# Second cross attention: a pair's residual, moments and normalisation on ScalarE and GpSimd instead of VectorE

## The reference, cut to what matters

```python
def _L1_xattn_ref(x, context, ln_gamma, ln_beta, w_q, w_kv, w_out, b_out, gate):
    xn = _layernorm(x, ln_gamma, ln_beta)
    q = (xn @ w_q).reshape(B, SQ, 16, 64)
    k, v = jnp.split(context @ w_kv, 2, axis=-1)      # then split into 16 heads
    attn = softmax(einsum('bqhd,bkhd->bhqk', q * SCALE, k))
    out = einsum('bhqk,bkhd->bqhd', attn, v).reshape(B, SQ, INNER)
    out = out @ w_out + b_out
    return out * jnp.tanh(gate[0])

x = _layernorm(x + _L1_xattn_ref(x, ctx_1024, ...))
```

## Time and profile before

| what | value |
|---|---|
| device time, median of 3 runs | 1886.55 us (1885.76 to 1887.1) |
| the profiled execution: device time / span | 1884.88 us / 1883.0 us |
| PE busy | 1667.1 us (89%) |
| DVE busy | 1549.9 us (82%) |
| ACT busy | 1275.3 us (68%) |
| POOL busy | 925.5 us (49%) |
| first to last `maximum` (L2217) of this phase | 603.7 to 1676.4 us |

### The profile page before, as it was taken

How to read it: one execution, slowest core, us unless ns; L and a number is a source line. 1 busy time by engine, 2 the same in 40 slices (tenths; PEclk the granted TensorE clock), 3 DMA queues, 4 the chain that set the end, 5 groups by cost and what they waited for, 6 DMA issues and landing times. The chain is left out here.

```text
span 1883.0 us, 34675 instructions
## 1 busy us (share of the span) xinstructions
PE 1667.1 (89%) x10425; PEld 1009.4 (54%) x10425; DVE 1549.9 (82%) x2885; ACT 1275.3 (68%) x2106; POOL 925.5 (49%) x723
## 2 busy tenths in 40 slices
PE   4987996889957899999999999999999999994997
PEld 2654665777733344554554554454455455454886
DVE  2765785877758999999999999999999999975887
ACT  2442332877735887887888788788788888864554
POOL 3640111363335766565665656656567465421333
PEclk9997998799978999999999999999999999997998
DMA  5203884311100898988899898898888889973231
GB/s 190 95 0 127 306 332 173 85 42 45 45 34 17 180 197 174 199 182 179 190 183 190 183 190 187 178 195 182 179 199 179 188 183 185 182 135 122 47 79 29
DMA packets 632266, 281.85 MB, mean 150 GB/s; under 512 B 601852, under 2 KB 606236, under 8 KB 631452
## 3 DMA queue, kind: packets, MB, share of 16 engines
q1 hardware_dynamic: 632204, 281.10, 64.2%
HBM read 129.02 MB, written 1.05 MB: 69 GB/s over the span
## 5 line engine op out<-in xcount | busy, mean ns | idle before, releaser
L2237 DVE SCALAR_TENSOR_TENSOR xa_h<-xa_psum,xa_rinv,xa_h 128x500 f16<-128x500 f32 x672 | 452.8, 730 | 1.0 <-ACT xa_h L2445 0.7
L2445 ACT ACTIVATE xa_h<-xa_psum,xa_rinv 128x1000 f16<-128x1000 f32 x448 | 371.5, 883 | 51.8 <-DVE xa_rinv L2228 51.5
L2429 ACT ACTIVATE xa_psum<-xa_psum,xa_bias,unscale_s 128x1500 f32<-128x1500 f32 x224 | 353.2, 1577 | 7.4
L2073 PE MATMUL xa_psum<-xa_c_hi,xa_q_hi 128*128 128x500 f16 x672 | 257.4, 383 | 54.5 <-DVE xa_h L2237 50.1
L2217 DVE TENSOR_REDUCE xa_psum<-xa_psum 128x1 f32<-128x1000 f32 x224 | 269.3, 1202 | 14.2 <-PE xa_psum L2075 13.4
L2098 PE MATMUL xa_psum<-xa_prT,xa_n_hi 128*128 128x512 f16 (+1 forms) x768 | 270.8, 353 | 3.6 <-issue 1.6
L2100 PE MATMUL xa_psum<-xa_prT,xa_n_lo 128*128 128x512 f16 (+1 forms) x768 | 270.6, 352 | 0.0
L2099 PE MATMUL xa_psum<-xa_prT,xa_n_hi 128*128 128x512 f16 (+1 forms) x768 | 270.6, 352 | 0.0
L2074 PE MATMUL xa_psum<-xa_c_lo,xa_q_hi 128*128 128x500 f16 x672 | 252.7, 376 | 0.0
L2075 PE MATMUL xa_psum<-xa_c_hi,xa_q_lo 128*128 128x500 f16 x672 | 252.4, 376 | 0.0
L1939 POOL TENSOR_SCALAR xa_ctxT<-xa_ctxT,scales 128x1500 f32<-128x1500 f32 x31 | 126.3, 4073 | 166.4 <-DMA xa_ctxT<-in_ctxT 166.4
(11 more groups left out here) (328 smaller groups left out, 3630.4 us busy)
## 6 DMA issues: line engine op xcount, KB each, us to landing
ctxN<-in_ctxP SPq DMA_DIRECT2D x16, 1536.0 KB, 9.5
xa_ctxP<-in_ctxP SPq DMA_DIRECT2D x32, 768.0 KB, 4.3
ctxT<-in_ctxT SPq DMA_DIRECT2D x16, 1500.0 KB, 6.4
xa_ctxT<-in_ctxT SPq DMA_DIRECT2D x32, 750.0 KB, 4.7
moe_spread<-weight_rows SPq DMA_DIRECT2D x16, 1024.0 KB, 8.4
xa_prT<-xa_h SPq DMA_TRANSPOSE x192, 5.5
up<-in_F_up SPq DMA_DIRECT2D x1, 2048.0 KB, 7.7
down<-in_F_down SPq DMA_DIRECT2D x1, 2048.0 KB, 11.8
```

What stands on the lines that cost most here:

```text
L2073: nc.tensor.matmul(out, qh, c_hi[:, b, a:z], start=True, stop=False)
L2237: nc.vector.scalar_tensor_tensor(low, psum[:, bank + a:bank + z, 0:W], rinv[:, s % 2, :], high, ALU.mult, ALU.subtract).then_inc(h2_ready, 1)
L2429: nc.scalar.activation(psum[:, bank:bank + 3, 0:W], psum[:, bank:bank + 3, 0:W], ACT.Exp, bias=bias[:, s % 2, :], scale=k.unscale_s[:, :], ...
L2445: nc.scalar.activation(h[:, H_SLOT[s], 0, a * W:z * W].rearrange("p (a c) -> p a c", c=W), psum[:, bank + a:bank + z, 0:W], ACT.Identity, ...
```

## The change

DVE's residual, moments and normalisation go. In their place:

- POOL makes xg earlier: `gated(i - 1)` stands behind `split_n(i, 0)` now, ahead of `scale_c(i + 1, 0)`.
- ACT at step 7 sums xg (`sum_x`), at step 9 scales y by the gate from PSUM into `yg` and sums it (`gate`), at step 11 squares r - mean and sums that (`square`). Each stands between exponentials(s) and high_part(s).
- POOL adds r = yg + xg and makes the negated mean (`residual`); then var + eps, its power -1/2, and xn itself (`normalise`), followed by the copy as before, all of it behind `split_n(i, 1)` and ahead of `scale_c(i + 1, 1)`.
- PE's turn at step 10 waits for ACT's `yg_ready` in place of DVE's `r_ready` before it overwrites the bank of y.

```diff
             def gated(i):
                 pool.wait_ge(bias_ready, 1)
                 pool.wait_ge(t.r_ready, last(i))
+                pool.sem_inc(gating, 1)
+                pool.wait_ge(x_sum_ready, last(i))
                 pool.tensor_tensor(xg[:, :, :], k.x_tok[:, bass.ds(i, 1), :], gated_bias[:, :].unsqueeze(1), ALU.add)\
                     .then_inc(xg_ready, 1)
+            def residual(i):
+                pool.wait_ge(yg_ready, this(i))
...
+                pool.tensor_tensor(t.r[:, :, :], yg[:, :, :], xg[:, :, :], ALU.add).then_inc(t.r_ready, 1)
+                pool.wait_ge(x_sum_ready, this(i))
+                pool.sem_inc(gating, 1)
+                pool.tensor_scalar(neg_mean[:, :], y_sum[:, :], x_sum[:, :], -1.0 / D, ALU.add, ALU.mult)\
+                    .then_inc(neg_mean_ready, 1)
+            def normalise(i):
+                pool.wait_ge(squares_ready, this(i))
...
+                pool.tensor_scalar(t.var_eps[:, 0, :], squares[:, :], 1.0 / D, k.eps[:, :], ALU.mult, ALU.add)\
+                    .then_inc(t.var_eps_ready, 1)
+                pool.wait_ge(t.var_eps_ready, this(i))
...
+                pool.tensor_tensor(t.rstd[:, 0, :], t.var_eps[:, 0, :], k.minus_half[:, :], ALU.pow).then_inc(t.rstd_ready, 1)
...
+                pool.tensor_scalar(t.xn[:, 0, :], t.r[:, 0, :], neg_mean[:, :], t.rstd[:, 0, :], ALU.add, ALU.mult)\
+                    .then_inc(t.xn_ready, 1)
+                t.pool_store(pool, i, 0)
...
                 split_n(i, 0, first)
+                if not first:
+                    gated(i - 1)
...
                 split_n(i, 1)
                 if not first:
-                    gated(i - 1)
-                    t.pool_rstd(pool, i - 1, 0)
-                    t.pool_store(pool, i - 1, 0)
+                    residual(i - 1)
+                if not first:
+                    normalise(i - 1)
...
                 if u == TURNED[0] and r == 1 and not first:
-                    pe.wait_ge(t.r_ready, this(i - 1))
+                    pe.wait_ge(yg_ready, this(i - 1))
...
-            def residual(i):
-
-                dve.wait_ge(y_ready, this(i))
-                dve.wait_ge(xg_ready, this(i))
-                nc.vector.scalar_tensor_tensor(t.r[:, 0, :], psum[:, 7, 0:128], k.gate_tanh[:, :], xg[:, 0, :],
-                                               ALU.mult, ALU.add).then_inc(t.r_ready, 1)
-                t.vector_moments(dve, i, 0)
...
-                        t.vector_normalise(dve, i - 1, 0)
...
+            def sum_x(i):
+                act.wait_ge(xg_ready, this(i))
...
+                nc.scalar.activation(yg[:, 0, :], xg[:, 0, :], ACT.Identity, accum_out=x_sum[:, :]).then_inc(x_sum_ready, 1)
+            def gate(i):
+                act.wait_ge(y_ready, this(i))
+                act.wait_ge(x_sum_ready, this(i))
+                nc.scalar.activation(yg[:, 0, :], psum[:, 7, 0:128], ACT.Identity, scale=k.gate_tanh[:, :],
+                                     accum_out=y_sum[:, :]).then_inc(yg_ready, 1)
+            def square(i):
+                act.wait_ge(t.r_ready, this(i))
+                act.wait_ge(neg_mean_ready, this(i))
...
+                nc.scalar.activation(yg[:, 0, :], t.r[:, 0, :], ACT.Square, bias=neg_mean[:, :],
+                                     accum_out=squares[:, :]).then_inc(squares_ready, 1)
...
             def step(i, s, first=False, end=False):
                 exponentials(i, s)
+                if s == min(OUTPUT) and not first:
+                    sum_x(i - 1)
+                if s == max(OUTPUT) and not first:
+                    gate(i - 1)
+                if s == SQUARES and not first:
+                    square(i - 1)
```

More of the change, by code:

```diff
@@ L1734, in state_cross_phase @@
         on = sb("on", [128, H1, 2, SP])
-        gated_bias, xg = sb("gated_bias", [128, D]), sb("xg", [128, 1, D])
+        gated_bias, xg, yg = sb("gated_bias", [128, D]), sb("xg", [128, 1, D]), sb("yg", [128, 1, D])
+        y_sum, x_sum, neg_mean, squares = (sb(n, [128, 1]) for n in ("y_sum", "x_sum", "neg_mean", "squares"))
         psum = ctx.enter_context(nc.psum_tensor("xa_psum", [128, 8, 512], fp32))
@@ L1752, in state_cross_phase @@
         on_zeroed, y_ready, bias_ready, xg_ready = sem("on_zeroed"), sem("y_ready"), sem("bias_ready"), sem("xg_ready")
+        yg_ready, x_sum_ready, sum_ready = sem("yg_ready"), sem("x_sum_ready"), sem("sum_ready")
+        neg_mean_ready, squares_ready, gating = sem("neg_mean_ready"), sem("squares_ready"), sem("gating")
         two_ready = sem("two_ready")
@@ L1864, in _ @@
             t.open_pool(pool)
+            open_sems(pool, 1, t.r_ready, t.xn_ready, neg_mean_ready)
             open_sems(pool, 1, xg_ready)
@@ L1998, in _ @@
             gated(PAIRS - 1)
-            t.pool_rstd(pool, PAIRS - 1, 0)
-            t.pool_store(pool, PAIRS - 1, 0)
+            residual(PAIRS - 1)
+            normalise(PAIRS - 1)
         @block.tensor
@@ L2198, in epilogue @@
                     outputs(i, part)
-                pe.wait_ge(t.r_ready, this(i))
+                pe.wait_ge(yg_ready, this(i))
                 t.tensor_transpose(pe, i, 0, psum[:, 7, 128:256])
@@ L2210, in _ @@
             open_sems(dve, NR, *turn_kept.values())
-            t.open_vector(dve)
+            open_sems(dve, 1, t.logits_kept)
             def maximum(i, s):
@@ L2260, in step @@
                     keep_turned(*at)
-                if s == RESIDUAL and not first:
-                    residual(i - 1)
                 maximum(i, s)
@@ L2382, in epilogue @@
                 keep_turned(i, TURNED[1], 2)
-                residual(i)
-                t.vector_normalise(dve, i, 0)
                 t.vector_logits(dve, i, 0, psum[:, 7, 0:E])
@@ L2394, in _ @@
             open_sems(act, NG, on_kept)
+            open_sems(act, 1, x_sum_ready, yg_ready, squares_ready)
             t.open_scalar(act)
+            def sum_x(i):
+                act.wait_ge(xg_ready, this(i))
+                act.wait_ge(squares_ready, last(i))
+                act.wait_ge(neg_mean_ready, last(i))
+                nc.scalar.activation(yg[:, 0, :], xg[:, 0, :], ACT.Identity, accum_out=x_sum[:, :]).then_inc(x_sum_ready, 1)
[7 more added lines that the diff above has]
+                act.wait_ge(neg_mean_ready, this(i))
+                act.wait_ge(t.var_eps_ready, last(i))
+                nc.scalar.activation(yg[:, 0, :], t.r[:, 0, :], ACT.Square, bias=neg_mean[:, :],
+                                     accum_out=squares[:, :]).then_inc(squares_ready, 1)
             def evacuate(i, g):
@@ L2515, in epilogue @@
                         evacuate(*at)
+                sum_x(PAIRS - 1)
+                gate(PAIRS - 1)
+                square(PAIRS - 1)
                 t.scalar_store(act, PAIRS - 1, 0, psum[:, 7, 128:256])
```

19 lines of the change are left out of this document (16 added, 3 removed).

## The result

| what | before | after |
|---|---|---|
| median | 1884.37 us (19 runs, 1881.77 to 1887.10) | 1880.82 us (19 runs, 1877.41 to 1886.64) |
| the profiled execution: time / span | 1884.88 / 1883.0 us | 1880.84 / 1878.0 us |
| busy DVE / ACT / POOL | 1549.9 / 1275.3 / 925.5 us | 1535.3 / 1288.8 / 943.5 us |
| first to last maximum of the phase | 603.7 to 1676.4 us | 604.9 to 1669.4 us |

The ratio is 0.998, with a 95% interval of 0.9973 to 0.9988: a little faster, as forecast (1879.5 us, 1873.5 to 1884.0). The gain is 3.6 us, where 7.0 had been forecast: the forecast time started from the median of three runs, 1886.55 us, and nineteen runs have 1884.37.

What follows compares the result with a forecast made beforehand. The DVE and ACT loop bounds most steps, PE steps 8 to 10. Step 10 gives -8.4 us, pair 15's end +1.4, sum -7.0: from 1886.55 to 1879.5 us, range 1873.5 to 1884.

Steps and rivals of the forecast that it cites:

- The gain at step 10: Without DVE's residual and moments maximum(10) starts 0.58 us a pair earlier, PE's scores allowing no more; 8.4 us in all.
- the rival of the full gain: PE does not cap step 10, so the full 0.96 us a pair comes: -13.0 us, 1873.5 us; chance 0.12.
- The normalisation at 0: At step 11 DVE's normalisation (0.34 us) lies beside a wait for ACT's sum, so its removal gives 0.
- PE late by 0.25 at step 11: PE can follow DVE's 0.58 us only by 0.33 before scores(11), but maximum(11) hardly waits for PE; 0.58 kept.
- ACT at 0: ACT's three new pieces, 0.5 us each, fit the 0.48 us wait in front of high_part: cost 0.
- The new chain at 0: From square(11) over POOL to xn, ready at 1202.8 instead of 1200.77; 1.25 us of slack before scores(13): cost 0.
- transpose released by POOL: Sign that would show the forecast wrong: PE's transpose at step 12 waits for POOL, with scores(13) late.
- The end of pair 15: Nothing covers the chain in the last pair: 3.7 us instead of 2.29, +1.4 us (from +0.9 to +3.2).
- PE not made up: PE's 0.25 us lateness at step 11 stays, leaving 0.33 us a pair: -3.4 us, 1883.2 us; chance 0.10.
- PE's limit isn't there: Modelled matmul ends put PE's scores(10) too late; the full 0.96 us a pair comes: 1873.5 us; chance 0.12.
- POOL beside DVE: Three more POOL instructions a pair slow DVE's copies of turned probabilities; 9 us come back: 1888.5 us; chance 0.05.
- The chain is too long: The ACT and POOL chain delays PE's transpose at step 12, ahead of scores(13); at 5 us 1902.7 us; chance 0.07.

Runs made afterwards that it cites:

- the two controls: Kernels before and after, each run once more without an edit: 1883.85 us (0.9996) and 1878.60 us (0.9966), ratios to the kernel before.
- the six adds: The changed kernel with six more POOL adds of 128x128 between the power and the normalisation: ratio 1.0047 to the kernel before.
- the thinned product: Kernels before and after, each without 13 of 16 matmul calls of PE's output product (steps 7 to 9): 0.9899 and 0.9841 to before.

## Why the prediction was right, point by point

**The gain at step 10**: right, with its reason. Forecast 0.58 a pair out of the 1.06 that went from DVE, measured 5.54 - 4.96 = 0.58, and 0.57 between the two controls. Maximum(10) is released by PE 0.50 us after the reciprocal's end, 0.04 after the modelled end of PE's piece as forecast, and without PE's work the full amount comes. That amount is 1.13 and not my 0.96, so the rival of the full gain was priced too low: 15 times 0.17 = 2.6 us further down than 1873.5. Over all pairs it is 8.4 us, as forecast, though pair 1 alone gave 0.79, for which I had no term. Where DVE's work went follows: half of the residual became a wait, and the normalisation had stood beside one.

**The normalisation at 0**: right, by the run that moved it alone: 0.015 us a pair, 0.2 in all.

**PE late by 0.25 at step 11**: right that this costs nothing. From maximum(10) to maximum(11) it is 5.00 to 5.01 us, as before. PE is late by 0.09 only: scores(11) starts at 1191.03, 2.82 us after maximum(10), where it was 2.73. The 0.33 us of waiting were counted from a modelled end of the turn, and PE starts its next matmul before such an end: scores(11) 0.45 us after the start of the turn (1190.58), which is given as 0.61 us long.

**ACT at 0**: right. `sum_x`, `gate` and `square` take 0.39, 0.45 and 0.48 us from the start of the activation to the end of its read, I took 0.5; `gate` waits for y in pair 15 only. The wait in front of high_part vanishes at steps 9 and 11, and shrinks to 0.19 us at step 7.

**The new chain at 0**: right in the cost, though less was left than I reckoned with. From the start of `square` to the end of xn I worked out 2.2 us, and it takes 1199.84 - 1197.18 = 2.66. The normalisation was cheaper than my 0.6 (0.44), the handing over dearer than 0.1: 0.31 from ACT's read to var + eps, 0.18 to the power, 0.40 to xn. Of the 1.25 us of slack 0.46 were so used, and the transpose, which I had 0.4 us clear of xn, came 0.18 us late: that much of the sign "transpose released by POOL" came true, but scores(13) was not late. The run with the six adds found 1.0 us still left, so the chain could be 3.7 us long, where I had 2.2 + 1.25 = 3.45.

**The end of pair 15**: the right direction, the term undersized by the same handing over. Forecast 1.4, measured 5.91 - (1705.24 - 1701.23) = 1.9, the logits' copy of before standing at 1705.24; against the second execution of before it is 2.2, with the 0.35 us of PE's clock. From y to the end of xn it is 4.16 us instead of the 3.7 worked out; 1.24 of it is between instructions, where six times 0.1 was taken.

**The period**: 66.96 measured, 66.95 forecast. That is closer than the working deserves: the first profile of before was 0.1 us a pair slow, and one step grew by 0.12 that no term of mine had. Both are nearly of one size and cancel in the period, not in the gain: 0.46 a pair instead of 0.58. The sum by the controls is -8.4 (step 10) + 1.9 (the loop's place) - 0.2 (the normalisation) = -6.7 up to the last maximum, where 6.7 was measured, and with the end -4.5 to -4.8 instead of -7.0. By the medians it is -3.6 and -5.9.

**The time**: 1880.82 us measured, 1879.5 forecast. This is nearer than the gain, and in part luck. The start of the sum, 1886.55 us from three runs, was 2.2 us above the median of nineteen; from 1884.37 the same sum gives 1877.4. The 3.6 us of the first comparison lie just outside the -4 to -10 to which I gave 0.66, the 5.9 of the second inside. Two terms fell short: the end of pair 15 by 0.5 to 0.8 us, and the place of the loop, 1.9 us, which I had not thought of.

**Slips in the working.** In the case of PE not made up, 15 times 0.33 less 1.4 is -3.6 and not -3.4. The lower bound of pair 15's end is +1.1 by its own terms and not +0.9. Maximum(11) was put near 1196.4 by the mean step; it stands at 1196.57, since that step has a copy in it and takes 5.02 us. None of them touches the forecast.

**The rivals.** *PE's limit isn't there*: fell, with the thinned product. *PE not made up*: fell, by the step at 11. *POOL beside DVE*: fell; the 96 copies of the turned probabilities took 670 to 693 ns, as in the earlier trace rows. The Trainium skill (GPSIMD Engine Reference, section 8) says that GpSimd and VectorE share SBUF interfaces. No run here shows a cost of it: three POOL instructions more a pair left those copies as they were. *The chain is too long*: real from 1.0 us on, and not reached.

## What to carry to other kernels

- Before taking work from the busiest engine, look at what releases the instruction behind it. Of 1.06 us that went, 0.58 counted, because the data of another engine came 0.5 us later; this was readable from one observed start and the end of one matmul.
- A chain that alternates between engines costs its handing over, up to 0.4 us each here, and it counts in full where nothing covers it. A prologue or an epilogue may keep the short form while the loop takes the one that spreads the work.
- When steps are compared one by one, also compare the one into the loop and the one over its branch. The lowest median is that of the change with pair 15's end on DVE and four increments ahead of DVE's loop: 1875.21 us, 0.9945 (0.9924 to 0.9966). Its interval overlaps the 0.9948 to 0.9976 of the same kernel without the increments, so only the traces set the two apart.
- A forecast of a time is its start plus a change. With three runs for the start, an error there of 2.2 us stood beside a gain of 3.6 to 5.9.

## What was not expected of the hardware

- A loop's first instructions can be 0.13 us late for its place in an engine's program alone: 0.23 us between reciprocal and copy instead of 0.10, changed by one instruction ahead of the loop. On the way into the loop they were 0.35 us late.
- On POOL a 128x128 operation with two per-row operands took 0.44 us as add and multiply and 0.80 as subtract and multiply, with the subtrahend in a two-element tile. Adds of 128x128 took 0.45 us alone and 0.36 in a row of six.
- ACT's accumulator read of 0.19 us starts some 0.1 us before its activation ends, so activation and read of 128 columns take 0.39 to 0.48 us together.
- Executions of one kernel differ by an even slowness, too: 67.53 and 67.43 us a pair in two profiles of the kernel before. A difference of 0.1 us a pair needs a control.
